# Opening of an attention-and-experts kernel: order of the first loads, constant products on TensorE, an early Sqrt, and quad 0 before quad 1's statistics

## The chip, the cores and the metric

The kernel runs on one core of a Trainium2 chip. The core has five engines that run their own instruction streams and meet at semaphores: TensorE (PE, with its weight loads shown as PEld), VectorE (DVE), ScalarE (ACT), GpSimd (POOL) and SyncE (SP, which here only issues loads and stores). The metric is device time in microseconds (us); the median of several executions counts.

## What is computed

One pre-norm transformer layer on x of shape (4, 1024, 128), float32: attention without softmax, then a mixture of 16 experts of which each token takes one, beside a shared expert.

```python
x = x + attn(layernorm(x))      # q, k l2-normed per head (16 heads of 8)
#   sim = q k^T / n**sigmoid(m[head]);  out = (sim v) Wo + bo
x = x + ffn(layernorm(x))       # router: top 1 of 16, score = sigmoid(top logit)
#   routed: (up * silu(gate)) down of the chosen expert; shared: silu(h Wg) * (h Wu) Wd
```

Since there is no softmax, (q k^T) v is computed as q (k^T v): a 128x128 matrix per sequence, masked to its head blocks.

## The kernel before

The 4096 rows are 32 tiles of 128 rows, and four tiles make a quad (8 quads, `Q = 4`). Everything stays in SBUF. Each engine has its own list of calls, in an order written out by hand; a call waits for the semaphores of what it reads or overwrites, and nothing behind it on its engine can pass it. So the order of the lists is the schedule.

The opening has these steps; c is the quad, h the half of it (two tiles).

- Loads. SP issues, per quad, `xT` (x transposed, for the products, L231) and `xres` (rows of x, for the statistics and the residual, L232), and after those of quad 0 the bias rows `b_qkv` (L234); behind the eight quads come the shared expert's weights. ACT issues `m_col` (L441), `w_qkv` (a centring matrix and Wq, Wk, Wv side by side, L442), `w_o` (L443), `bo_in` (L444) and `rwT`, the router (L445).
- Head scaling. ACT takes an Exp of `m_col` (L449), DVE two small steps (L923, L924), ACT a second Exp (L451). DVE's `scale_mask` (L909) multiplies it into `head_mask`.
- Centred weights. PE's `center_weights` (L1119) multiplies the centring matrix with the weights as soon as `w_qkv` has landed, and ACT copies the product to `w_c` (L454).
- Statistics. DVE's `x_stats(c)` (L726, L729) gives mean and variance per row, ACT's `std_x(c)` (L460) the root, DVE's `x_scales(c)` (L739) its reciprocal.
- Projection. PE's `project(c, h)` (L1135) multiplies two tiles of `xT` by `w_c` into two of four PSUM banks; one float32 product is two passes in the trace. DVE's `take(c, h)` (L764) scales them by the row's factor, adds `b_qkv` and writes `qkv`. The next quad's half can be projected only when the take of the same half has emptied its banks.
- Head norms. ACT's `square(c)` (L492), DVE's `head_sums(c)` (L772), ACT's `head_norms(c)` (L496, L500), DVE's `inv_norms(c)` (L777). Then POOL scales v and q (`scale_v`, `scale_q`, L322), and PE forms k^T v (`v_by_k`, L1144) and turns q (`turn_q`, L1161). `qkv` has two slots, so `take(2, 0)` needs both of quad 0's.

Then follow, interleaved by hand over the quads, the attention output (`fold_wo`, `attend`), the second layer norm, the router, the ranks of the rows within their expert (`choose`, `place`), POOL's scatter of the rows to DRAM by expert, the gather of 48 tiles of expert rows, the experts' products, POOL's scatter back, and the shared expert, which fills gaps to the end.

The call lists around the change, before it: ACT runs `std_x(0)`, `std_x(1)`, `square(0)`, `std_x(2)`, `head_norms(0)`, `square(1)`, `head_norms(1)` (L550 to L556). DVE runs `x_stats(0)`, `bias_rows`, `scale_mask`, `x_stats(1)`, `x_scales(0)`, `take(0, 0)`, `x_scales(1)`, `take(0, 1)`, `x_stats(2)`, `take(1, 0)`, `head_sums(0)`, `take(1, 1)`, `x_scales(2)`, `inv_norms(0)`, `head_sums(1)`, `x_stats(3)`, `inv_norms(1)`, `take(2, 0)` (L925 to L942). PE runs `center_weights`, `project` of quads 0 to 2, `v_by_k(0)`, `turn_q(0)`, `v_by_k(1)`, `turn_q(1)`, `project(3, 0)` (L1302 to L1313).

Of the kernel before, what the change touches and what calls it, by code (L numbers as in the profile page):

```python
# [8 lines left out]
ACT = mybir.ActivationFunctionType  # L9
# [5 lines left out]
P = 128  # L15


def build_block(nc, S, x, x_t, w_in, b_in, Wo, bo, m_col_in, router_t, gate_up, down, shared_gate, shared_up,
# [4 lines left out]
    _, NT, D = x.shape  # L23
    HEADS = 16
    HD = D // HEADS
    _, E, F2 = gate_up.shape
# [26 lines left out]
    with ExitStack() as ctx:  # L53
# [62 lines left out]
        with ExitStack() as attention:  # L116
            def sb_a(name, shape, dt=F32):
                return attention.enter_context(nc.sbuf_tensor(name, shape, dt))

            qkv = sb_a("qkv", [P, QRING, Q, QKV])  # L120
            sq = sb_a("sq", [P, Q, 2 * D])
            xT = sb_a("xT", [P, T])
            qT = sb_a("qT", [P, RING, Q * P])
            ss = sb_a("ss", [P, 2, Q, 2 * HEADS])
            rn = sb_a("rn", [P, 2, Q, 2 * HEADS])
            vkm = sb_a("vkm", [P, 2, D])
            wb = sb_a("wb", [P, 2, D])
            w_qkv = sb_a("w_qkv", [P, D + QKV])
            b_qkv = sb_a("b_qkv", [P, QKV])
            w_c = sb_a("w_c", [P, QKV])  # L130
            m_col = sb_a("m_col", [P, 1])
            m_tmp = sb_a("m_tmp", [P, 4])
            head_mask = sb_a("head_mask", [P, D])
            zeros = sb_a("zeros", [P, E, W])
            w_sh = sb_a("w_sh", [P, 2, SF])
            bo_in = sb_a("bo_in", [2, D])
            bo_top = sb_a("bo_top", [2, D], F32R)
            bo_two = sb_a("bo_two", [2, Q, D], F32R)
            two_col = sb_a("two_col", [2, 1])
            ones_r = sb_a("ones_r", [2, P], F32R)  # L140
# [86 lines left out]

        @block.sync
        def _(sp):
            for c in range(NQ):  # L230
                sp.dma_start(xT[:, 512 * c:512 * c + 512], x_t[:, 512 * c:512 * c + 512]).then_inc(ld_xt[c], 16)  # L231
                sp.dma_start(xres[:, Q * c:Q * c + Q, :], x[:, Q * c:Q * c + Q, :]).then_inc(ld_x[c], 16)  # L232
                if c == 0:
                    sp.dma_start(b_qkv[:], b_in.partition_broadcast(P)).then_inc(ld_b, 16)  # L234
            sp.dma_start(w_sh[:, 0], shared_gate).then_inc(ld_sg, 16)
            sp.dma_start(w_sh[:, 1], shared_up).then_inc(ld_su, 16)

            sp.wait_ge(z_done, 2)
            heads_of = x_slots.rearrange("(e r) d -> r e d", e=E)
            sp.dma_start(heads_of[0:P], zeros[:]).then_inc(zero_st, 16)  # L240
            sp.dma_start(sdT[:], shared_down).then_inc(ld_sd, 16)
            sp.dma_start(w_gu[:], gate_up).then_inc(ld_wg, 16)
            sp.dma_start(w_dn[:], down).then_inc(ld_wd, 16)

            def load(g):
                first = slot_values(0, g, mybir.EngineType.SP, E * REG - P)
                if g == 0:
                    sp.wait_ge(zero_st, 16)
                    for landed in scat:
                        sp.wait_ge(landed, 16 * NT // 2)  # L250
                for j in range(Q):
                    sp.dma_start(xg[:, g * Q + j, :], x_slots[bass.ds(first[j], P), :]).then_inc(xg_ld[g], 16)  # L252

            def bring(c):
                if c == 0:
                    for turn, landed in enumerate(y_sent):
                        sp.wait_ge(landed, 16 * len(range(turn, SLOTS, 3)))
                sp.dma_start(y_rows[:, Q * c:Q * c + Q, :], by_place[:, Q * c:Q * c + Q, :]).then_inc(y_ld[c], 16)

            sp.wait_ge(table_rdy, 1)  # L260
            for g in range(NG):
                load(g)
            for c in range(NQ):
                bring(c)
            for c in range(0, NQ, 2):
                sp.wait_ge(fin, c + 1)
                sp.dma_start(out[:, Q * c:Q * c + Q, :], xres[:, Q * c:Q * c + Q, :]).then_inc(out_st, 16)
            sp.wait_ge(fin, NQ + 1)
            sp.dma_start(out[:, Q * LAST + 2:NT, :], xres[:, Q * LAST + 2:NT, :]).then_inc(out_st, 16)
            sp.wait_ge(out_st, 16 * (NQ + 1))  # L270
# [168 lines left out]
        def _(act):  # L439
            a = nc.scalar  # L440
            act.dma_start(m_col[:], m_col_in).then_inc(ld_m, 16)  # L441
            act.dma_start(w_qkv[:], w_in).then_inc(ld_wa, 16)  # L442
            act.dma_start(w_o[:], Wo).then_inc(ld_wo, 16)  # L443
            act.dma_start(bo_in[:], bo.partition_broadcast(2)).then_inc(ld_bo, 16)  # L444
            act.dma_start(rwT[:], router_t).then_inc(ld_rw, 16)  # L445

            act.wait_ge(ld_m, 16)
            act.wait_ge(k_col, 1)
# [1 line left out]
            act.wait_ge(m_step, 1)  # L450
            a.activation(m_tmp[:, 3:4], m_tmp[:, 2:3], ACT.Exp, bias=zero_col[:],  # L451
                         scale=-float(np.log(S))).then_inc(ach, 1)
            act.wait_ge(wc_mm, 1)
            a.copy(w_c[:], pair[:, 0, 0:QKV]).then_inc(wc_rdy, 1)  # L454
            act.wait_ge(k_id, 1)

            def std(dst, mv, var, done, c):
                t = slice(Q * c, Q * c + Q)
# [3 lines left out]
            def std_x(c):  # L462
                std(rs1, mv1, var1, std1, c)
# [24 lines left out]
            def square(c):  # L488
                act.wait_ge(qkv_sb, 2 * (c + 1))
                if c >= 1:  # L490
                    act.wait_ge(ssum, c)
                a.activation(sq[:], qkv[:, c % QRING, :, 0:2 * D], ACT.Square).then_inc(sq_done, 1)  # L492

            def head_norms(c):
                act.wait_ge(ssum, c + 1)
                a.activation(ss[:, c % 2], ss[:, c % 2], ACT.Relu, bias=floor_neg[:], scale=1.0).then_inc(floored, 1)  # L496
                if c >= 2:
                    act.wait_ge(q_rdy, c - 1)
                act.wait_ge(floored, c + 1)
                a.activation(rn[:, c % 2], ss[:, c % 2], ACT.Sqrt, bias=floor_col[:], scale=1.0).then_inc(nrm, 1)  # L500
# [47 lines left out]
                a.copy(yg[:, g % YRING], ps_yg[:].rearrange("p (j d) -> p j d", d=D)).then_inc(yg_rdy, 1)  # L548

            std_x(0)  # L550
            std_x(1)
            square(0)
            std_x(2)
            head_norms(0)
            square(1)
            head_norms(1)  # L556
            qT_copy(0)
# [157 lines left out]
        def _(dve):  # L715
# [16 lines left out]
            def x_stats(c):  # L732
                dve.wait_ge(ld_x[c], 16)
                stats(c, st1, mv1, var1)
# [190 lines left out]
            x_stats(0)  # L925
            bias_rows()
            scale_mask()
            x_stats(1)
            x_scales(0)
            take(0, 0)  # L930
            x_scales(1)
            take(0, 1)
            x_stats(2)
            take(1, 0)
            head_sums(0)
            take(1, 1)
            x_scales(2)
            inv_norms(0)
            head_sums(1)
            x_stats(3)  # L940
            inv_norms(1)
# [171 lines left out]
        @block.tensor  # L1113
        def _(pe):
            te = nc.tensor

            def center_weights():
                pe.wait_ge(ld_wa, 16)
# [171 lines left out]
            def down_experts(g, after=None):  # L1290
# [8 lines left out]
                                   stop=True)  # L1299
                mm.then_inc(e_dn_mm, 1)  # L1300

            center_weights()  # L1302
            project(0, 0, after=(wc_rdy, 1))
            project(0, 1)
            project(1, 0, after=(qkv_sb, 1))
# [219 lines left out]
```

## Time and profile before

| | us |
|---|---|
| median of 3 runs (213.49 to 215.41) | 214.48 |
| the profiled execution, whole | 215.95 |
| its span, first to last instruction | 214.0 |

The profile is one execution. Its span leaves out about 2 us that lie around it, and its whole time is 0.7% over the median. Over the span PE is busy 90%, DVE 69%, ACT 48% and POOL 52%, but the share changes from stage to stage: what an edit is worth is read from its own stage.

### The profile page before, as it was taken

The numbers are of one execution on the slowest core, as the hardware profiler recorded it, in microseconds if no ns is written. First come the engines' busy times: TensorE is split into PE (matmuls) and PEld (weight loads), VectorE is DVE, ScalarE is ACT, GpSimd is POOL, SyncE is SP. The second block draws the span as 40 slices with busy tenths as digits, with TensorE's granted clock in tenths as the row PEclk, the third lists the DMA queues.
The fourth block names the chain that finished last, engine by engine and source line by source line (L and its number), as shares of the span: only waits on it lengthen the run. The fifth ranks groups of instructions, "written<-read, shape, count | busy, mean of one in ns | idle before, by whom it ended". The sixth has DMA issues, their size and how long they took to land.

```text
span 214.0 us, 3828 instructions
## 1 busy us (share of the span) xinstructions
PE 191.9 (90%) x1126; PEld 155.4 (73%) x1126; DVE 146.9 (69%) x502; ACT 103.0 (48%) x234; POOL 112.2 (52%) x140
## 2 busy tenths in 40 slices
PE   0597599999989899999888999999999999979994
PEld 0253466665768576798767988899999898869883
DVE  4759999999999977866726577856635334236555
ACT  3315265793658299683412558546653222222230
POOL 6000703347599876668740057757777778770000
PEclk9999999999999999999999999999999999999999
DMA  5999991000110011111124446621110110008525
GB/s 167 311 390 261 217 420 54 3 2 12 39 40 26 25 37 40 39 45 42 50 53 112 101 122 159 157 63 43 39 42 29 44 47 12 1 7 276 212 85 209
DMA packets 17751, 21.59 MB, mean 101 GB/s; under 512 B 3240, under 2 KB 11951, under 8 KB 17476
## 3 DMA queue, kind: packets, MB, share of 16 engines
q1 hardware_dynamic: 14016, 15.87, 25.6%
q0 software_dynamic: 2560, 4.24, 6.2%
q10 hardware_dynamic: 1156, 1.26, 1.7%
q8 instruction: 9, 0.15, 0.3%
q14 instruction: 10, 0.08, 0.1%
HBM read 13.95 MB, written 8.44 MB: 105 GB/s over the span
## 4 chain that ended last, share of the span: by engine, by line
PE 34%; DVE 27%; POOL 13%; issue 9%; DMA 9%; SPq 5%; ACT 1%; POOLq 1%; ACTq 0%; DVEq 0%
DVE qkv L764 7%; POOL y_back L357 7%; PE quad_banks L1279 6%; POOL x_slots L348 5%; SPq L252 4%; PE bank L1298 4%; DMA x_slots<-h_rows,pos 4%; DVE ss L772 4%; DVE st L726 4%; PE bank L1242 3%; DMA w_qkv<-w_in 3%; PE quad_banks L1220 3%; PE quad_banks L1222 3%; PE quad_banks L1221 3%; PE quad_banks L1135 2%
## 5 line engine op out<-in xcount | busy, mean ns | idle before, releaser
L357 POOL DMA_INDIRECT y_back<-yg,xg x48 | 47.3, 986 | 31.0 <-ACT yg L548 16.6
L849 DVE TENSOR_TENSOR s_act<-quad_banks,sg_act 128x512 f32<-128x512 f32 x32 | 22.0, 689 | 27.6 <-PE bank L1242 13.8
L520 ACT ACTIVATE sg_act<-quad_banks 128x512 f32<-128x512 f32 x32 | 19.2, 599 | 44.0 <-PE quad_banks L1222 44.0
L348 POOL DMA_INDIRECT x_slots<-h_rows,pos x32 | 31.7, 991 | 12.8 <-issue 6.3
L322 POOL TENSOR_TENSOR qkv<-qkv,rn 128x512 f32<-128x512 f32 x16 | 17.1, 1080 | 29.2 <-DVE rn L777 29.0
L1242 PEld LDWEIGHTS bank<-sdT,s_act 128*128 128x128 f32 x224 | 28.0, 191 | 1.5
L1242 PE MATMUL bank<-sdT,s_act 128*128 128x128 f32 x224 | 28.9, 275 | 0.0
L1135 PE MATMUL quad_banks<-w_c,xT 128*128 128x384 f32 x64 | 25.5, 533 | 2.1 <-DVE qkv L764 1.3
L1279 PE MATMUL quad_banks<-w_gu,xgT 128*128 x96 | 22.9, 382 | 0.8 <-ACT xgT L531 0.8
L1135 PEld LDWEIGHTS quad_banks<-w_c,xT 128*128 128x128 f32 x64 | 12.2, 208 | 11.2 <-issue 3.8
L1279 PEld LDWEIGHTS quad_banks<-w_gu,xgT 128*128 128x128 f32 x96 | 17.3, 190 | 2.9 <-issue 1.0
L764 DVE SCALAR_TENSOR_TENSOR qkv<-quad_banks,rs,b_qkv 128x384 f32<-128x384 f32 x32 | 17.7, 603 | 2.2 <-PE quad_banks L1135 2.2
L539 ACT ACTIVATE eg_act<-quad_banks,esc 128x128 f32<-128x128 f32 x48 | 13.7, 371 | 9.5 <-PE quad_banks L1279 8.7
L895 DVE SCALAR_TENSOR_TENSOR e_act<-quad_banks,esc,eg_act 128x128 f32<-128x128 f32 x48 | 13.5, 344 | 6.9 <-ACT eg_act L539 6.9
L1220 PE MATMUL quad_banks<-hT,sgT 128*128 128x512 f32 x32 | 14.8, 462 | 2.8 <-DVE s_act L849 1.6
L726 DVE BATCH_NORM_STATS2 st<-xres 128x6 f32<-128x128 f32 x64 | 13.7, 276 | 1.3 <-DMA xres<-L_attn_x 1.2
L476 ACT ACTIVATE h_rows<-xres,nm,rs 128x128 f32<-128x128 f32 x32 | 13.2, 484 | 2.0 <-DVE nm L750 2.0
L904 DVE COPY e_actT<-bank 128x512 f32<-128x512 f32 x12 | 8.3, 689 | 7.7 <-PE bank L1287 7.7
L332 POOL TENSOR_TENSOR hT<-hT_full,hT 128x512 fp32r<-128x512 f32 x8 | 10.7, 1356 | 3.8 <-ACT hT L486 3.7
L1298 PEld LDWEIGHTS bank<-w_dn,e_actT 128*128 128x128 f32 x96 | 12.3, 191 | 0.5
L1298 PE MATMUL bank<-w_dn,e_actT 128*128 x96 | 12.7, 275 | 0.0
L1221 PE MATMUL quad_banks<-hT,suT 128*128 128x512 f32 x32 | 12.6, 395 | 0.0
(146 smaller groups left out, 373.5 us busy)
## 6 DMA issues: line engine op xcount, KB each, us to landing
xg<-x_slots SPq DMA_DIRECT2D x48, 65.0 KB, 1.9
xT<-x_t SPq DMA_DIRECT2D x8, 256.0 KB, 6.8
xres<-L_attn_x SPq DMA_DIRECT2D x8, 256.0 KB, 7.0
w_gu<-gate_up SPq DMA_DIRECT2D x1, 2048.0 KB, 14.0
h_rows<-y_back SPq DMA_DIRECT2D x8, 256.0 KB, 5.3
x_slots<-zeros SPq DMA_DIRECT2D x1, 1040.0 KB, 15.4
w_dn<-down SPq DMA_DIRECT2D x1, 1024.0 KB, 15.9
out<-xres SPq DMA_DIRECT2D x4, 256.0 KB, 2.4
```

The source lines that it names most:

```text
L348: g.indirect_dma_start(out=x_slots, out_offset=bass.IndirectOffsetOnAxis(ap=pos[:, t:t + 1], axis=0), in_=h_rows[:, t, :], in_offset=None) ...
L357: nc.gpsimd.indirect_dma_start(out=y_back, out_offset=bass.IndirectOffsetOnAxis(ap=xg[:, n, D + 1:D + 2].bitcast(I32), axis=0), in_=yg[:, ...
L520: a.activation(sg_act[:, n % 2], pair[:, 2 * (n % 2)], ACT.Silu).then_inc(s_silu, 1)
L726: last = v.bn_stats(st[:, t, :], xres[:, t, :])
L764: last = v.scalar_tensor_tensor(out=qkv[:, c % QRING, j, :], in0=pair[:, j, 0:QKV], scalar=rs1[:, t:t + 1], in1=b_qkv[:], op0=ALU.mult, op ...
L849: v.tensor_tensor(s_act[:, n % 2], pair[:, 2 * (n % 2) + 1], sg_act[:, n % 2], ALU.mult).then_inc(s_act_rdy, 1)
L1135: last = te.matmul(pair[:, j, 0:QKV], xT[:, P * (Q * c + j):P * (Q * c + j + 1)], w_c[:], start=True, stop=True)
L1220: te.matmul(to, lhs[:, 0], rhs[:, 0], start=True, stop=False)
L1221: te.matmul(to, lhs[:, 0], rhs[:, 1], start=False, stop=False)
L1242: last = te.matmul(Y_BANK[c][:, here], s_act[:, n % 2, here], sdT[:, D * k:D * k + D], start=(k == 0 and j == 0), stop=(k == KC - 1 and j ...
L1279: mm = te.matmul(gate_up_banks(g % 2)[:, j, :], xgT[:, g % 2, P * j:P * j + P], gu_cols[:, bass.ds(held[g][j] * 2, F2)], start=True, stop= ...
L1298: mm = te.matmul(ps_yg[:, here], e_actT[:, g % 2, here], dn_cols[:, bass.ds(cols[j], D)], start=True, stop=True)
```

## The change

- SP issues `w_qkv` first and no longer `b_qkv`. ACT issues `m_col`, then `b_qkv` and `bo_in`; it issues `w_o` and `rwT` only behind the copy of `w_c`.
- ACT calls a Sqrt of one column, whose value nothing reads, behind its second Exp and ahead of the copy of `w_c`. `m_tmp` is one column wider for it. The wait for `k_id` moves with it.
- PE multiplies `ones` by `ones` into a bank that nothing uses yet: four products before `center_weights`, one behind it. It waits for `k_pool`, the memsets, first.
- ACT's `square(0)` comes ahead of `std_x(1)`, and `head_norms(0)` ahead of `std_x(2)`.
- DVE takes quad 0 ahead of `x_stats(1)`; `head_sums(0)`, `take(1, 0)`, `inv_norms(0)` and `take(1, 1)` come ahead of `x_stats(2)`. From `x_stats(3)` on the order is as before.

```diff
--- before.py
+++ after.py
@@ -129,7 +129,7 @@
             b_qkv = sb_a("b_qkv", [P, QKV])
             w_c = sb_a("w_c", [P, QKV])
             m_col = sb_a("m_col", [P, 1])
-            m_tmp = sb_a("m_tmp", [P, 4])
+            m_tmp = sb_a("m_tmp", [P, 5])
             head_mask = sb_a("head_mask", [P, D])
             zeros = sb_a("zeros", [P, E, W])
             w_sh = sb_a("w_sh", [P, 2, SF])
@@ -227,11 +227,10 @@
 
         @block.sync
         def _(sp):
+            sp.dma_start(w_qkv[:], w_in).then_inc(ld_wa, 16)
             for c in range(NQ):
                 sp.dma_start(xT[:, 512 * c:512 * c + 512], x_t[:, 512 * c:512 * c + 512]).then_inc(ld_xt[c], 16)
                 sp.dma_start(xres[:, Q * c:Q * c + Q, :], x[:, Q * c:Q * c + Q, :]).then_inc(ld_x[c], 16)
-                if c == 0:
-                    sp.dma_start(b_qkv[:], b_in.partition_broadcast(P)).then_inc(ld_b, 16)
             sp.dma_start(w_sh[:, 0], shared_gate).then_inc(ld_sg, 16)
             sp.dma_start(w_sh[:, 1], shared_up).then_inc(ld_su, 16)
 
@@ -439,10 +438,8 @@
         def _(act):
             a = nc.scalar
             act.dma_start(m_col[:], m_col_in).then_inc(ld_m, 16)
-            act.dma_start(w_qkv[:], w_in).then_inc(ld_wa, 16)
-            act.dma_start(w_o[:], Wo).then_inc(ld_wo, 16)
+            act.dma_start(b_qkv[:], b_in.partition_broadcast(P)).then_inc(ld_b, 16)
             act.dma_start(bo_in[:], bo.partition_broadcast(2)).then_inc(ld_bo, 16)
-            act.dma_start(rwT[:], router_t).then_inc(ld_rw, 16)
 
             act.wait_ge(ld_m, 16)
             act.wait_ge(k_col, 1)
@@ -450,9 +447,12 @@
             act.wait_ge(m_step, 1)
             a.activation(m_tmp[:, 3:4], m_tmp[:, 2:3], ACT.Exp, bias=zero_col[:],
                          scale=-float(np.log(S))).then_inc(ach, 1)
+            act.wait_ge(k_id, 1)
+            a.activation(m_tmp[:, 4:5], zero_col[:], ACT.Sqrt, bias=eps_col[:], scale=1.0)
             act.wait_ge(wc_mm, 1)
             a.copy(w_c[:], pair[:, 0, 0:QKV]).then_inc(wc_rdy, 1)
-            act.wait_ge(k_id, 1)
+            act.dma_start(w_o[:], Wo).then_inc(ld_wo, 16)
+            act.dma_start(rwT[:], router_t).then_inc(ld_rw, 16)
 
             def std(dst, mv, var, done, c):
                 t = slice(Q * c, Q * c + Q)
@@ -548,10 +548,10 @@
                 a.copy(yg[:, g % YRING], ps_yg[:].rearrange("p (j d) -> p j d", d=D)).then_inc(yg_rdy, 1)
 
             std_x(0)
+            square(0)
             std_x(1)
-            square(0)
+            head_norms(0)
             std_x(2)
-            head_norms(0)
             square(1)
             head_norms(1)
             qT_copy(0)
@@ -925,17 +925,17 @@
             x_stats(0)
             bias_rows()
             scale_mask()
-            x_stats(1)
             x_scales(0)
             take(0, 0)
+            take(0, 1)
+            x_stats(1)
+            head_sums(0)
             x_scales(1)
-            take(0, 1)
+            take(1, 0)
+            inv_norms(0)
+            take(1, 1)
             x_stats(2)
-            take(1, 0)
-            head_sums(0)
-            take(1, 1)
             x_scales(2)
-            inv_norms(0)
             head_sums(1)
             x_stats(3)
             inv_norms(1)
@@ -1114,6 +1114,10 @@
         def _(pe):
             te = nc.tensor
 
+            def warm(n):
+                for _ in range(n):
+                    te.matmul(ps_log[:, 0:P], ones[:], ones[:], start=True, stop=True)
+
             def center_weights():
                 pe.wait_ge(ld_wa, 16)
                 te.matmul(pair[:, 0, 0:QKV], w_qkv[:, 0:D], w_qkv[:, D:D + QKV], start=True, stop=True
@@ -1299,7 +1303,10 @@
                                    stop=True)
                 mm.then_inc(e_dn_mm, 1)
 
+            pe.wait_ge(k_pool, 1)
+            warm(4)
             center_weights()
+            warm(1)
             project(0, 0, after=(wc_rdy, 1))
             project(0, 1)
             project(1, 0, after=(qkv_sb, 1))
```

## Rows read from the trace of the kernel before

**Rows 1.** Windows: us, busy of PE, PEld, DVE, ACT, POOL, granted clock, DMA share, GB/s.

```profile
14.00:24.55 10.55, 8.21 (x30) 4.18 (x28) 9.64 (x28) 4.48 (x8) 2.12 (x2) 1.00 1.19 254
24.55:74.80 50.25, 46.36 (x249) 32.96 (x250) 48.72 (x179) 30.22 (x68) 30.04 (x30) 1.00 0.21 79
```

**Rows 2.** Chain of waits: start us, us, what.

```profile
1.25 5.93 DMA w_qkv<-w_in
```

**Rows 3.** Timeline of ACT: start, us, engine, line, operation, tiles, count, [idle before, releaser].

```profile
5.25 0.29 ACT L451 ACTIVATE m_tmp<-m_tmp,zero_col 128x1 f32<-128x1 f32 x1 [0.42 <-DVE m_tmp L924]
...
8.91 0.48 ACT L454 COPY w_c<-quad_banks 128x384 f32<-128x384 f32 x1 [3.37 <-PE quad_banks L1119]
9.40 1.28 ACT L460 ACT_TABLE_LOAD   x1
10.70 0.49 ACT L460 ACTIVATE rs<-mv,eps_col 128x4 f32<-128x4 f32 x2
...
15.79 1.06 ACT L492 ACTIVATE sq<-qkv 128x1024 f32<-128x1024 f32 x1 [4.60 <-DVE qkv L764]
```

**Rows 4.** Timeline of PE, in narrow windows so that single passes show.

```profile
7.22 1.65 PE L1119 MATMUL quad_banks<-w_qkv 128*128 128x384 f32 x2 [7.22 <-DMA w_qkv<-w_in]
9.53 0.98 PE L1135 MATMUL quad_banks<-w_c,xT 128*128 128x384 f32 x1 [0.66 <-ACT w_c L454]
...
12.86 1.39 PE L1135 MATMUL quad_banks<-w_c,xT 128*128 128x384 f32 x2
13.50 1.07 PE L1135 MATMUL quad_banks<-w_c,xT 128*128 128x384 f32 x2
14.09 0.81 PE L1135 MATMUL quad_banks<-w_c,xT 128*128 128x384 f32 x2
...
25.73 1.16 PE L1144 MATMUL bank<-qkv 128*128 128x128 f32 x8 [1.69 <-POOL qkv L322]
26.77 0.66 PE L1161 MATMUL bank<-ident,qkv 128*128 128x128 f32 x4
27.26 1.46 PE L1135 MATMUL quad_banks<-w_c,xT 128*128 128x384 f32 x4
```

**Rows 5.** Timeline of DVE up to the first take.

```profile
5.31 0.87 DVE L726 BATCH_NORM_STATS2 st<-xres 128x6 f32<-128x128 f32 x4
...
6.83 0.21 DVE L914 CAST ones_r<-ones 2x128 fp32r<-2x128 f32 x1 [0.23 <-DMA bo_in<-L_attn_bo]
...
8.13 0.27 DVE L909 TENSOR_SCALAR head_mask<-head_mask,m_tmp 128x128 f32<-128x128 f32 x1
...
11.03 0.18 DVE L739 RECIPROCAL rs<-rs 128x4 f32<-128x4 f32 x1 [0.17 <-ACT rs L460]
12.57 1.14 DVE L764 SCALAR_TENSOR_TENSOR qkv<-quad_banks,rs,b_qkv 128x384 f32<-128x384 f32 x2 [1.36 <-PE quad_banks L1135]
```

**Rows 6.** Timeline of DVE from the second take of quad 0 on.

```profile
14.62 1.14 DVE L764 SCALAR_TENSOR_TENSOR qkv<-quad_banks,rs,b_qkv 128x384 f32<-128x384 f32 x2 [0.82 <-PE quad_banks L1135]
15.68 0.86 DVE L726 BATCH_NORM_STATS2 st<-xres 128x6 f32<-128x128 f32 x4
...
16.87 1.11 DVE L764 SCALAR_TENSOR_TENSOR qkv<-quad_banks,rs,b_qkv 128x384 f32<-128x384 f32 x2
17.89 1.21 DVE L772 TENSOR_REDUCE ss<-sq 128x128 f32<-128x1024 f32 x1
...
23.61 0.92 DVE L777 RECIPROCAL rn<-rn 128x128 f32<-128x128 f32 x1
24.55 1.14 DVE L764 SCALAR_TENSOR_TENSOR qkv<-quad_banks,rs,b_qkv 128x384 f32<-128x384 f32 x2
```

**Rows 7.** Timeline of SP's queue, the first issue.

```profile
0.81 0.39 SPq L231 DMA_DIRECT2D xT<-x_t  x1
```

**Rows 8.** By line, L231: the landing of that load.

```profile
DMA to landing us min/median/max: 3.3/3.3/3.3
```

## The prediction

> **What bounds the kernel now.** I read the windows first, then the timeline of each engine over the opening, then the landing of the loads. From the start of take(2,0) at 24.55 us to 74.80 us VectorE (DVE) is busy 48.72 of 50.25 us [rows 1]. Whatever reaches VectorE in that stretch earlier or later moves what follows by nearly as much, and the order behind take(2,0) is not edited. At that point both orders have done the same VectorE work. So the change is worth the shift of the start of take(2,0), and I call it S.
>
> The opening before 24.55 has two parts. Up to the first take at 12.57 us VectorE waits: w_qkv lands at 1.25 + 5.93 = 7.18 us [rows 2], TensorE centres the weights, ScalarE (ACT) copies w_c at 8.91, and the products of quad 0 start at P0 = 9.53 [rows 3, 4]. The first take starts 3.04 us behind P0 and the second 5.09 us behind it (14.62) [rows 5, 6]. From the end of that second take, where the next operation starts at T = 15.68, VectorE is almost solid, and take(2,0) starts 8.87 us later [rows 6].
>
> The products of quad 0 run slow. One pass of 384 columns starts 0.64 us behind the other (12.86, 13.50), while from 14.09 on, and later (four in 1.46 us), the pace is about 0.32 us [rows 4]. The granted-clock column reads 1.00 over both stretches [rows 1], so it is the pace that tells the level: 1.2 GHz up to about 14.0 us and 2.4 GHz after. Before that rise TensorE had worked without a pause since 9.53, that is for some 4.5 us.
>
> **The change part by part.**
>
> *Weights first on SP.* The first xT load, as large as w_qkv, was issued at 0.81 [rows 7] and landed 3.3 us later [rows 8]; from that place w_qkv lands at about 4.1. The centre product takes 1.65 us [rows 4] and is ready at about 5.8. xT and xres of quad 0 each move one place back on SP, while xT of quad 1 and all that follow keep their place, since b_qkv leaves the third. b_qkv goes second on ACT's queue.
>
> *When xres of quad 0 lands.* Call this Lx. Before, x_stats(0) started at 5.31 [rows 5], so it had landed by then; a later place gains nothing, and 5.3 is the lower bound. The upper one is 7.2, the landing of w_qkv, which had the second place on the other queue [rows 2]. I take the middle, 6.3, as the new third place lies between. Behind it VectorE needs x_stats(0) 1.29 (5.31 to 6.60, as 6.83 follows 0.23 of idle), bias_rows 1.30, scale_mask 0.27 and x_scales(0) 0.18 [rows 5]: VectorE is free for the first take at about Lx + 3.1 = 9.4 (8.4 to 10.3).
>
> *Root table early.* ScalarE's second Exp ends at 5.25 + 0.29 = 5.54. Now the table load of Sqrt follows it: 1.28 us, to 6.83, and the small Sqrt some 0.2 before the next instruction can start (two of them take 0.49) [rows 3]. The copy of w_c stands behind both, so it starts at about 7.05, although its product is ready at 5.8. P0 follows the copy's start by 0.62 (8.91 to 9.53) [rows 3, 4]: the new P0 is 7.67, and not the 6.45 that the weights would allow. An Exp up to 0.2 earlier would take as much off. The load is only moved: it stood at 9.40, beside products that the first take had to await anyway, so 1.2 us of the gain is spent here. A landing of w_qkv anywhere up to 5.3 gives the same P0. The Trainium skill's "ScalarE: Activation LUTs", section "What ACT_TABLE_LOAD costs", counts 1.28 us for the load and 1.38 us more for a drain. By that rule P0 would be 9.05 and the sum below 216.4; the trace does not agree, since the load starts 0.01 us behind the copy and the next instruction 0.02 us behind the load [rows 3], and I go by the trace.
>
> *Loads moved behind the copy.* ScalarE issues w_o and rwT before std_x(0), at about 0.4 us each by an issue on SP [rows 7], so std_x(0) starts near 8.4. This is hidden by VectorE's bias_rows and scale_mask, which run to about 9.2; both loads are first needed behind take(2,0). Without that cover it costs 0.8. SP issues as many loads as before.
>
> *Constant products.* Four products on ones, then one behind the centre product. Their 128 columns are a third of the 384 of a pass, so by the slow pace a pass takes 0.21 us and four products of two passes 1.7 us. They fill 1.7 to 3.5 us, before w_qkv lands, and the fifth fits into the wait for the copy. They cost nothing; the question is whether they raise the clock. After them TensorE stands idle from about 6.0 to 7.67. I take the row of before: idle or in pieces until the projections, then about 4.5 us at the slow rate, and the products of quad 0 as far behind P0 as they were.
>
> *The new order of VectorE.* take(0,0) then starts at 7.67 + 3.04 = 10.7, take(0,1) at 7.67 + 5.09 = 12.76, and T is 13.8. Behind T, with steps from start to start [rows 6]: x_stats(1) 1.19, head_sums(0) 1.13, x_scales(1) 0.1, take(1,0) 1.04, inv_norms(0) 0.93, take(1,1) 1.04, x_stats(2) 1.19, which is 6.62. square(0), 1.06 [rows 3], is done under x_stats(1), and head_norms(0) under take(1,0): each of its two steps has 128 columns, so it takes no longer than the w_c copy's 0.48 on 384 [rows 3]. Now VectorE waits: std_x(2) can start only after x_stats(2), and ScalarE's square(1) stands behind std_x(2) although its input has been ready for 1.2 us. std_x(2) starts at about 6.73, square(1) at 6.95 and ends at 8.0, so head_sums(1) starts at 8.04. Then 1.13, x_stats(3) 1.2 and inv_norms(1) 0.94: take(2,0) starts at T + 11.3. Before it was T + 8.87. Of the 2.4 more, 1.2 is x_stats(1), which used to fill the wait for the products, 0.1 x_scales(1), and 1.1 the new wait.
>
> **Sum.** S = (13.8 + 11.3) - 24.55 = +0.55. The break-even is T = 13.25. Against the profiled execution this is a span of 214.6 for 214.0. Its own whole time, 215.95, lies 0.7% over the median, 214.48; on the median the sum gives 215.0.
>
> **The rivals.**
>
> *The clock is up before quad 0's products.* Then the products are ready at P0 + 1.5 and P0 + 2.8, VectorE becomes the bound at Lx + 3.1, and T is 11.6 (at the earliest 11.55, by the second half; with Lx = 7.2 it is 12.4). S is -1.65, from -1.7 to -0.85: 212.8, up to 213.6. For it: TensorE would be at work for about 3.8 of the 4.2 us from 1.7 to 5.9. Against it: the pause to 7.67, and that 1.65 us of centre product did not do it before. By the Trainium skill's "TensorE: Matmul & The Clock Gate", Part 1, the slow clock is the default and sustained activity releases it; the trace agrees as far as the rise at 14.0 goes.
>
> *The clock falls in a new pause (slower).* Behind project(2,1), which waits for take(1,1) and ends near T + 7.05, TensorE has v_by_k(0), 1.16, and turn_q(0), 0.66 [rows 4], and is idle from about T + 8.9. v_by_k(1) follows the end of inv_norms(1) by 1.18 (24.55 to 25.73), so it starts at T + 12.5: a pause of 3.6 us, where before it was 1.69 and four passes behind it still took 1.46 [rows 4]. If the clock falls there, the work of the next 4.5 us (v_by_k(1), turn_q(1), project(3)) runs at half pace and loses at most 2.25, less some slack: with +0.55 that is 216.0 to 217.3, say 216.8. It decides only if the clock falls in that pause; it did not in the one of 1.69, and no row here shows a longer one after the rise.
>
> *The early landing fails (slower).* If ACT's and SP's loads share so that w_qkv lands at 7.18 as before, P0 stays 9.53, T is 15.7 and S +2.4: 216.9. It decides from a landing at 5.3 on. Against it stands the xT load from the same place.
>
> **How the numbers follow.** The forecast, with the clock rising during quad 0's products, has 0.52. If the rise comes 1.5 us earlier, T is 0.75 less; if it comes only after them, T is about 0.5 more: 214.3 to 215.6. The early clock has 0.28, the pause 0.10, the late landing 0.04, and 0.06 is left for what I don't see, on either side. The range leaves out the outer ends: 212.8, the low end of the early clock, to 216.6. A change of 1%, or 2.1 us, is about what a measurement of this kernel can tell from none. Faster than 212.3 needs more than the early clock gives by the sum: 0.10. Slower than 216.6 is the larger part of the pause and the late landing: 0.10. Within 1%: 0.80.
>
> **What the profile will show.** Right: w_qkv's centre product at 4.1 to 4.3; ScalarE's table load between 5.4 and 6.9 and the w_c copy right behind it; P0 near 7.7; passes 0.64 apart in quad 0's first half; square(1) behind std_x(2), with two idle stretches of VectorE of 0.4 and 0.8 us; take(2,0) near 25.1. Wrong: 0.32 us passes from the start with take(2,0) near 23; or slow passes again behind the pause; or a w_c copy that does not wait for the table.

## The result and the profile after

| | before | after |
|---|---|---|
| median of 4 executions, us | 214.94 (213.49 to 215.5) | 217.82 (216.89 to 218.17) |
| the profiled execution, whole | 215.95 | 216.89 |
| its span | 214.0 | 215.0 |
| start of take(2,0) in it | 24.55 | 24.92 |

The ratio after to before is 1.0138, 95% interval 1.0073 to 1.0202: the change made the kernel slower by 2.9 us. A second set of after, beside other executions of before, gave 217.8 and 1.013 (1.0051 to 1.0209). Forecast were 215.0 and a range up to 216.6. The profiled execution of before was one of its slower ones and that of after its fastest, so the two spans show 1.0 of the 2.9. In the comparisons below single executions that lie over 1.5% above the fastest of their kernel are left out of the ratio; medians are over all.

The page of after, two lines: the span, and the granted clock in 40 slices of 5.4 us.

```profile
span 215.0 us, 3848 instructions
PEclk9889979999999999999999999999999999999999
```

The clock falls twice, around 9 and around 26 us; before it stood at 1.00 in the stretches of [rows 1]. The windows of after, columns as in [rows 1]:

```profile
4.00:7.00 3.00, 1.83 (x4) 1.03 (x4) 0.32 (x2) 2.47 (x5) 0.43 (x5) 1.00 0.67 170
...
9.00:12.00 3.00, 3.00 (x6) 1.33 (x4) 2.80 (x15) 0.30 (x1) 0.00 (x0) 0.50 1.07 396
...
24.00:26.00 2.00, 0.00 (x0) 0.00 (x0) 2.00 (x7) 0.51 (x2) 0.92 (x1) 1.00 1.15 247
26.00:28.00 2.00, 1.79 (x8) 1.79 (x9) 1.97 (x11) 0.30 (x1) 1.19 (x2) 0.50 1.01 404
28.00:30.00 2.00, 2.00 (x9) 1.65 (x8) 1.75 (x11) 0.82 (x2) 0.00 (x0) 0.65 0.99 418
```

TensorE does nothing from 24 to 26 us, and the clock is at half (1.2 GHz) right behind it. TensorE's timeline (start, us, engine, line, operation; in brackets the idle time before and what ended it):

```profile
1.80 2.08 PE L1119 MATMUL bank<-ones 128*128 128x128 f32 x8 [1.80 <-POOL seen L284]
3.93 1.65 PE L1123 MATMUL quad_banks<-w_qkv 128*128 128x384 f32 x2
5.37 0.45 PE L1119 MATMUL bank<-ones 128*128 128x128 f32 x2
...
7.93 1.93 PE L1139 MATMUL quad_banks<-w_c,xT 128*128 128x384 f32 x4 [2.10 <-DMA xT<-x_t]
...
9.01 3.40 PE L1139 MATMUL quad_banks<-w_c,xT 128*128 128x384 f32 x5
...
21.59 0.60 PE L1165 MATMUL bank<-ident,qkv 128*128 128x128 f32 x4
26.21 2.08 PE L1148 MATMUL bank<-qkv 128*128 128x128 f32 x8 [4.02 <-POOL qkv L321]
28.08 1.06 PE L1165 MATMUL bank<-ident,qkv 128*128 128x128 f32 x4
```

The constants and the centre product run ahead of 6 us, as planned, and the first products of quad 0 are fast: three passes from 7.93 to 9.01, 0.36 us each. From 9.01 on it is five in 3.40, 0.68 each. Later comes the pause, 4.02 us, and behind it `v_by_k(1)` takes 2.08 us for the 1.16 of before and `turn_q(1)` 1.06 for 0.66 [rows 4]. VectorE's timeline:

```profile
8.71 0.87 DVE L726 BATCH_NORM_STATS2 st<-xres 128x6 f32<-128x128 f32 x4 [3.95 <-DMA xres<-L_attn_x]
...
11.63 2.19 DVE L764 SCALAR_TENSOR_TENSOR qkv<-quad_banks,rs,b_qkv 128x384 f32<-128x384 f32 x4
13.74 0.86 DVE L726 BATCH_NORM_STATS2 st<-xres 128x6 f32<-128x128 f32 x4
...
20.81 0.18 DVE L739 RECIPROCAL rs<-rs 128x4 f32<-128x4 f32 x1 [0.36 <-ACT rs L460]
21.75 1.22 DVE L772 TENSOR_REDUCE ss<-sq 128x128 f32<-128x1024 f32 x1 [0.77 <-ACT sq L492]
...
24.92 1.04 DVE L764 SCALAR_TENSOR_TENSOR qkv<-quad_banks,rs,b_qkv 128x384 f32<-128x384 f32 x2
...
30.75 1.22 DVE L772 TENSOR_REDUCE ss<-sq 128x128 f32<-128x1024 f32 x1 [0.81 <-ACT sq L492]
31.89 1.66 DVE L764 SCALAR_TENSOR_TENSOR qkv<-quad_banks,rs,b_qkv 128x384 f32<-128x384 f32 x3
```

The first statistics wait till 8.71 for `xres` (5.31 before, [rows 5]); take(2,0) is 0.37 late against [rows 6]; take(3,0) starts at 31.89, so behind the slow stretch it is 1.44 late against this row of before:

```profile
30.45 2.18 DVE L764 SCALAR_TENSOR_TENSOR qkv<-quad_banks,rs,b_qkv 128x384 f32<-128x384 f32 x4
```

ScalarE's timeline, which answers to [rows 3]; ACTq is its queue of loads:

```profile
5.11 1.28 ACT L451 ACT_TABLE_LOAD   x1
5.62 0.35 ACTq L454 DMA_DIRECT2D w_o<-L_attn_Wo  x1
6.01 0.78 ACTq L455 DMA_DIRECT2D rwT<-router_t  x1
6.41 0.29 ACT L451 ACTIVATE m_tmp<-zero_col,eps_col 128x1 f32<-128x1 f32 x1
6.61 0.46 ACT L453 COPY w_c<-quad_banks 128x384 f32<-128x384 f32 x1
```

### The profile page after: what moved, and what is told of

It reads as the page before. It is cut to its first block, busy times and chain, and to the rows that moved or that the text cites. A ratio compares the mean times of both kernels' runs of the same rounds, so it can differ in the third digit from the quotient of the medians.

```text
span 215.0 us, 3848 instructions
## 1 busy us (share of the span) xinstructions
PE 194.8 (91%) x1136; PEld 158.7 (74%) x1136; DVE 146.2 (68%) x502; ACT 103.2 (48%) x235; POOL 112.2 (52%) x140
## 4 chain that ended last, share of the span: by engine, by line
PE 42%; DVE 13%; POOL 13%; DMA 11%; issue 8%; SPq 6%; ACT 1%; POOLq 0%; DVEq 0%
DMA x_slots<-h_rows,pos 10%; PE bank L1246 7%; POOL x_slots L347 7%; PE quad_banks L1283 6%; PE quad_banks L1224 5%; SPq L251 5%; PE quad_banks L1226 5%; PE quad_banks L1225 5%; PE bank L1302 4%; POOL qkv L321 4%; DVE qkv L764 3%; DVE st L726 3%; PE bank L1291 2%; PE bank L1257 2%; DVE ss L772 2%
## 5 line engine op out<-in xcount | busy, mean ns | idle before, releaser
L356 POOL DMA_INDIRECT y_back<-yg,xg x48 | 47.3, 985 | 29.2 <-ACT yg L548 13.9
L1139 PE MATMUL quad_banks<-w_c,xT 128*128 128x384 f32 x64 | 25.2, 527 | 4.8 <-DVE qkv L764 2.5
L1139 PEld LDWEIGHTS quad_banks<-w_c,xT 128*128 128x128 f32 x64 | 11.9, 203 | 13.0 <-issue 5.8
L764 DVE SCALAR_TENSOR_TENSOR qkv<-quad_banks,rs,b_qkv 128x384 f32<-128x384 f32 x32 | 17.5, 598 | 0.2
L726 DVE BATCH_NORM_STATS2 st<-xres 128x6 f32<-128x128 f32 x64 | 13.8, 277 | 4.2 <-DMA xres<-L_attn_x 4.0
L1224 PE MATMUL quad_banks<-hT,sgT 128*128 128x512 f32 x32 | 14.8, 463 | 1.5 <-DVE s_act L849 1.4
L1148 PE MATMUL bank<-qkv 128*128 128x128 f32 x64 | 9.5, 296 | 4.0 <-POOL qkv L321 4.0
L1226 PE MATMUL quad_banks<-hT,sgT 128*128 128x512 f32 x32 | 12.7, 396 | 0.0
```

What stands on the lines that cost most here:

```text
L356: nc.gpsimd.indirect_dma_start(out=y_back, out_offset=bass.IndirectOffsetOnAxis(ap=xg[:, n, D + 1:D + 2].bitcast(I32), axis=0), in_=yg[:, ...
L726: last = v.bn_stats(st[:, t, :], xres[:, t, :])
L764: last = v.scalar_tensor_tensor(out=qkv[:, c % QRING, j, :], in0=pair[:, j, 0:QKV], scalar=rs1[:, t:t + 1], in1=b_qkv[:], op0=ALU.mult, op ...
L1139: last = te.matmul(pair[:, j, 0:QKV], xT[:, P * (Q * c + j):P * (Q * c + j + 1)], w_c[:], start=True, stop=True)
L1224: te.matmul(to, lhs[:, 0], rhs[:, 0], start=True, stop=False)
L1226: return te.matmul(to, lhs[:, 1], rhs[:, 0], start=False, stop=True)
```

## The experiments

Two theories. The pause theory: take(2,0) comes about as late as the sum said, and the loss is the clock that falls in the pause of 4.02 us ahead of `v_by_k(1)`, which the new call order of VectorE made. The loads theory: the loss comes from the opening's loads, which land late (`xres` at 8.71). Both can hold, for different parts of the time.

All twelve, each beside the kernel before on the same chip; e1 to e4, e5 to e8 and e9 to e12 are three sets on three chips, so rows of different sets are best compared by their ratios to before. e5 is after once more. The pause is what remains of it where constants fill it. "Clock" is the mean granted clock of each execution: a recorded slow stretch such as the one from 26 to 30 us above takes off (0.50 x 2 + 0.35 x 2) / 215 = 0.008, so the figure counts the falls, wherever in the span they lie. It does not price them: before itself has at least one (0.990 to 0.992) in 18 of its 57 executions, and in e1 the three executions with one (214.19 to 215.00) are faster than the median of the other seven (215.68).

| kernel | median us | ratio to before (95%) | take(2,0) | pause ahead of v_by_k(1) | clock |
|---|---|---|---|---|---|
| after | 217.82 | 1.0138 (1.0073 to 1.0202) | 24.92 | 4.02 | 0.976 to 0.990 |
| e1_fill_pause | 215.12 | 1.0043 (1.0010 to 1.0076) | 24.87 | 0.90 | 0.998 and above in 7 of 10 |
| e2_calls_back | 215.79 | 1.0062 (1.0023 to 1.0101) | 23.63 | 1.69 | 0.998 and above in 5 of 10 |
| e3_loads_back | 215.62 | 1.0051 (1.0012 to 1.0089) | 24.39 | 2.79 | 0.983 to 0.992 |
| e4_bias_third | 212.41 | 0.9898 (0.9831 to 0.9965) | 22.24 | 2.68 | 0.976 to 0.992 |
| e5_after_again | 217.80 | 1.0130 (1.0051 to 1.0209) | 24.73 | 4.02 | 0.984 to 0.992 |
| e6_bias_rows | 216.14 | none | 24.03 | 2.79 | 0.976 to 0.992 |
| e7_calls_only | 218.70 | 1.0151 (1.0058 to 1.0244) | 25.68 | 4.02 | 0.976 to 0.992 |
| e8_all_three | 210.80 | 0.9816 (0.9719 to 0.9912) | 21.55 | 1.79 | 1.000, one 0.990 |
| e9_no_const | 218.06 | 1.0209 (1.0144 to 1.0274) | 25.74 | 4.02 | 0.976 to 0.991 |
| e10_bias_calls_back | 213.75 | 0.9989 (0.9952 to 1.0025) | 21.99 | 1.69 | below 0.993 in 7 of 10 |
| e11_no_fill | 214.14 | 0.9992 (0.9957 to 1.0027) | 21.39 | 1.91 | 0.984 to 0.992 |
| e12_calls_back_fill | 212.53 | 0.9901 (0.9861 to 0.9941) | 21.86 | 0.57 | 0.998 and above in 6 of 10 |

### The pause, filled

After, with 14 more constant products between `turn_q(0)` and `v_by_k(1)`.

```diff
             turn_q(0)
+            warm(14)
             v_by_k(1)
```

> The changed kernel with 14 more products of ones on TensorE between turn_q(0) and v_by_k(1), about 3.1 us of the 4.0 us pause at the fast rate. Theory PAUSE (the clock falls to 0.50 in that pause, and the half-rate stretch from 26.0 to 29.3 us is what was lost): granted clock 1.00 from 24 to 32 us, v_by_k(1) in about 1.1 us for 2.08, take(3,0) near 31.0 for 31.89, time 1.0 to 2.0 us under the changed kernel (216 to 217). Rival LOADS (the late landing of quad 0's xT and xres is the loss) and rival ORDER (the new call order of VectorE costs it by itself): clock or not, the time stays within 0.5 us of the changed kernel's 217.8.

TensorE's timeline of this kernel:

```profile
21.97 3.29 PE L1119 MATMUL bank<-ones 128*128 128x128 f32 x28
26.16 1.16 PE L1148 MATMUL bank<-qkv 128*128 128x128 f32 x8 [0.90 <-POOL qkv L321]
27.19 0.66 PE L1165 MATMUL bank<-ident,qkv 128*128 128x128 f32 x4
```

The added products compute nothing that is used, and 2.7 us come back by the medians (217.82 to 215.12), 2.0 by the ratios; 1.0 to 2.0 was expected. All ten executions (at most 216.72) are faster than all eight of after (at least 216.89). take(2,0) starts at 24.87 and `v_by_k(1)` at 26.16, both as late as in after, so nothing ahead of them has moved; it takes 1.16 us again, and take(3,0) starts at 30.67 for 31.89. This is the cleanest verdict of the study: the lost clock behind the pause is most of what made the change slow. What is left, +0.9 us by the ratio, is near the S of 0.55 that the sum gave.

### The call lists, taken back and taken alone

After with before's lists of DVE and ACT:

```diff
+            x_stats(1)
             x_scales(0)
             take(0, 0)
-            take(0, 1)
-            x_stats(1)
-            head_sums(0)
             x_scales(1)
...
```

> The changed kernel with the call lists of VectorE and ScalarE as before; its loads, constant products and early Sqrt stay. PAUSE: TensorE's pause ahead of v_by_k(1) is back at about 1.7 us, the clock stays up behind it, take(2,0) starts near 23.9 (x_stats(0) still late, at 8.7, then x_stats(1) ahead of the first take, T near 15.0, plus 8.9); time 214 to 215.2, some 3 us under the changed kernel. LOADS: x_stats(0) still starts at 8.7, so the time stays at 217 or more. ORDER: as PAUSE in time, but then the first run of this set (the filled pause) gains nothing.

And the other way round, before with only the new lists:

> The kernel before with nothing but the new call lists of VectorE and ScalarE. From the steps: T near 15.7 as before, then 11.2 to 11.3 to take(2,0), for 8.9: near 27, and a pause of TensorE of some 4 us ahead of v_by_k(1), with a recorded fall of the clock in most runs: 217.5 to 219.5, 3 to 5 us over before. If the constant products were needed for a fall, the clock stays at 1.00 and the time at 216.5 to 217.2.

The new lists alone make before slower by 1.5%: take(2,0) comes 1.1 us later, and they bring the pause of 4.02 and the half clock behind it (0.79 from 26 to 28 us, 0.50 from 28 to 30). So with before's loads that part of the change hurts. Taking it back did not bring all of it back, though: 215.79, above the 214 to 215.2 expected. TensorE's timeline of after with before's lists:

```profile
22.50 0.63 PE L1165 MATMUL bank<-ident,qkv 128*128 128x128 f32 x4
24.82 1.26 PE L1148 MATMUL bank<-qkv 128*128 128x128 f32 x8 [1.69 <-POOL qkv L321]
25.87 1.10 PE L1165 MATMUL bank<-ident,qkv 128*128 128x128 f32 x4
26.76 2.64 PE L1139 MATMUL quad_banks<-w_c,xT 128*128 128x384 f32 x4
```

Here the clock falls behind a pause of 1.69 us, the very length that left it up in before [rows 4]: four passes take 2.64, not 1.46. Five of the ten executions show no fall (median 215.0) and five do (216.5). So one profile with a pause and no fall did not show that such a pause is safe.

### The loads

After with before's order of loads on SP and ACT:

```diff
-            sp.dma_start(w_qkv[:], w_in).then_inc(ld_wa, 16)
...
+                if c == 0:
+                    sp.dma_start(b_qkv[:], b_in.partition_broadcast(P)).then_inc(ld_b, 16)
...
-            act.dma_start(b_qkv[:], b_in.partition_broadcast(P)).then_inc(ld_b, 16)
+            act.dma_start(w_qkv[:], w_in).then_inc(ld_wa, 16)
+            act.dma_start(w_o[:], Wo).then_inc(ld_wo, 16)
...
```

> The changed kernel with the loads on the queues and in the order of before; its call lists, constant products and early Sqrt stay. LOADS: quad 0's xT and xres land at 4 to 5.5 us again and the time comes back to 215 or less. PAUSE: w_qkv lands near 7.2, the projections start near 9.5, take(2,0) comes at 25.5 to 27, TensorE's pause of about 4 us and the half-rate stretch behind it stay; time 217.8 to 219.5, no better than the changed kernel.

2.2 us faster than after (1.9 by the ratios), so the new order of loads is no gain as it stands. The time lies between the two that were expected, and it does not separate the theories: take(2,0) is 0.5 us earlier than in after, take(3,0) 1.7, and the 1.2 between them is the clock, which stays up behind a pause of 2.79. TensorE's and then VectorE's timeline:

```profile
25.68 1.16 PE L1149 MATMUL bank<-qkv 128*128 128x128 f32 x8 [2.79 <-POOL qkv L322]
```

```profile
24.39 1.04 DVE L765 SCALAR_TENSOR_TENSOR qkv<-quad_banks,rs,b_qkv 128x384 f32<-128x384 f32 x2
...
30.19 2.18 DVE L765 SCALAR_TENSOR_TENSOR qkv<-quad_banks,rs,b_qkv 128x384 f32<-128x384 f32 x4
```

`w_qkv` landed at 5.5 us here, with the queues of before, where the profile of before has 7.18 [rows 2]; e7, with the same queues, has 5.6. The clock fell too, between 17 and 21 us, in quad 2's products, which the takes reach later: take(2,0) follows T by 11.17 us, as in after (11.18), so a fall there cost VectorE nothing up to that point.

The next one undoes a single line of the load order: `b_qkv` goes back to SP, behind quad 0's `xT` and `xres`, while `w_qkv` stays first.

```diff
                 sp.dma_start(xres[:, Q * c:Q * c + Q, :], x[:, Q * c:Q * c + Q, :]).then_inc(ld_x[c], 16)
+                if c == 0:
+                    sp.dma_start(b_qkv[:], b_in.partition_broadcast(P)).then_inc(ld_b, 16)
...
-            act.dma_start(b_qkv[:], b_in.partition_broadcast(P)).then_inc(ld_b, 16)
```

> The changed kernel with one load moved: b_qkv (a row broadcast to 128 partitions) is issued by SP behind quad 0's xT and xres, and no longer second by ACT. If the broadcast holds up what lands beside it: xT of quad 0 lands near 5.3 for 7.9, xres near 6 for 8.7, the projections start near 7.1 (behind the table load and the copy of w_c), take(2,0) 1 to 2 us earlier than 24.9. If it is only a matter of places in the queues, xT and xres gain less than 0.7 us. LOADS then sees the time at 215.5 or less; PAUSE sees the pause and the half-rate stretch stay and the time at 216 to 217.

TensorE's and then VectorE's timeline of it (one line added, so L1140 for L1139, L727 for L726, L765 for L764):

```profile
7.14 5.77 PE L1140 MATMUL quad_banks<-w_c,xT 128*128 128x384 f32 x16 [1.26 <-ACT w_c L454]
```

```profile
5.80 0.87 DVE L727 BATCH_NORM_STATS2 st<-xres 128x6 f32<-128x128 f32 x4 [1.11 <-DMA xres<-L_attn_x]
...
11.06 0.86 DVE L727 BATCH_NORM_STATS2 st<-xres 128x6 f32<-128x128 f32 x4
...
22.24 1.04 DVE L765 SCALAR_TENSOR_TENSOR qkv<-quad_banks,rs,b_qkv 128x384 f32<-128x384 f32 x2
...
28.04 2.18 DVE L765 SCALAR_TENSOR_TENSOR qkv<-quad_banks,rs,b_qkv 128x384 f32<-128x384 f32 x4
```

`xres` lands 2.9 us earlier (5.80), take(2,0) comes 2.7 earlier, and the kernel is 5.4 us faster than after (5.1 by the ratios) and 1.0% faster than before. That rests on three executions (212.07 to 212.47); the fourth took 217.56, at a clock of 0.976. Not all of the gain is the loads' own: take(3,0) is 3.9 us earlier than in after, and the 1.2 beyond the 2.7 is the fall, which is no longer there behind a pause of 2.68. The rest is not traced. Now the products wait for the copy of `w_c`, behind the table load, as the prediction had it; in after they waited for `xT`. A load of 192 KB that nothing needed before the first take (11.63 in after) had delayed those that everything waited for.

Is it the bytes or their pattern? `b_qkv` is one row of 1.5 KB that the load reads 128 times, once for each partition. In the next kernel it is laid out in DRAM as 128 equal rows, and its load stands where it stands in after, with the same bytes.

```diff
-            act.dma_start(b_qkv[:], b_in.partition_broadcast(P)).then_inc(ld_b, 16)
+            act.dma_start(b_qkv[:], b_in).then_inc(ld_b, 16)
```

> The changed kernel with b_qkv laid out in DRAM as 128 equal rows, so that its load reads 192 KB of different addresses, from the same place in the queue, in place of one row 128 times. Theory BROADCAST (reading one row 128 times is what is slow and holds up its neighbours): the moved GB/s from 4 to 7 us go from 170 to 300 or more, xT of quad 0 lands at 5.0 to 6.2 for 7.9, take(2,0) 1.5 to 2.7 us earlier than 24.9, time 213 to 215.5. Rival PLACE (any 192 KB there do the same): xT lands at 7.3 or later, and the time stays at 217 or more.

The loads issued from 0.5 to 2.5 us, first of after, then of this kernel (KB each, us from issue to landing), and then this kernel's window that answers to the 170 GB/s of after:

```profile
xres<-L_attn_x SPq DMA_DIRECT2D x1, 256.0 KB, 7.0
b_qkv<-b_in ACTq DMA_DIRECT2D x1, 192.0 KB, 6.8
```

```profile
xres<-L_attn_x SPq DMA_DIRECT2D x1, 256.0 KB, 4.5
b_qkv<-b_in ACTq DMA_DIRECT2D x1, 192.0 KB, 4.1
```

```profile
4.00:7.00 3.00, 2.08 (x4) 1.18 (x4) 1.11 (x6) 2.21 (x5) 0.41 (x5) 1.00 1.03 368
```

It is the pattern. With distinct rows `b_qkv` lands after 4.1 us, not 6.8, its neighbour `xres` after 4.5, not 7.0, and all queues together move 368 GB/s in these three microseconds, not 170 (five profiles with the broadcast in this place lie between 170 and 192). As a time this kernel tells little (213 to 215.5 was expected): two executions took 214.3 and 214.5, two 217.8 at a clock of 0.976, and in its profile quad 0's products ran slow again, so that take(2,0) stands at 24.03.

### The constants

After without its constant products:

```diff
-            pe.wait_ge(k_pool, 1)
-            warm(4)
             center_weights()
-            warm(1)
```

> The changed kernel without its constant products. If they are of little account where quad 0's xT lands at 7.9: the first products run slow, T moves from 13.7 to about 14.1, the pause ahead of v_by_k(1) stays and so does a recorded fall: 217.3 to 218.7 us. If they are what buys the falls (a clock raised early, then lost in the wait for xT): mean granted clock 0.992 or more in all runs and 215.5 to 217.

The window of this kernel that answers to 9 to 12 us of after:

```profile
9.00:12.00 3.00, 3.00 (x6) 1.49 (x6) 2.81 (x15) 0.30 (x1) 0.00 (x0) 1.00 1.07 395
```

Quad 0's products start at the same place, 8.00, and are slow from the first pass on, though the column reads 1.00; T is 14.56, 0.8 later than in after, and take(2,0) 25.74. So the constants do raise the clock ahead of the products, against what the prediction took. In time it is not to be told from after: the two intervals overlap. The late `xres` holds VectorE back either way, and the pause of 4.02 is there in both.

### All three, and what each is worth

`b_qkv` third on SP as above, `square(1)` ahead of `std_x(2)` on ScalarE, and short runs of constants in the three waits of TensorE:

```diff
-            std_x(2)
             square(1)
+            std_x(2)
...
-            warm(1)
+            warm(3)
             project(0, 0, after=(wc_rdy, 1))
...
+            warm(6)
             project(2, 0, after=(qkv_sb, 3))
...
+            warm(6)
             v_by_k(1)
```

> The changed kernel with b_qkv behind quad 0's loads on SP, square(1) ahead of std_x(2) on ScalarE, and constant products in TensorE's pauses: three for one behind center_weights, six ahead of project(2,0), six ahead of v_by_k(1). By the steps: take(2,0) 0.7 to 0.9 us ahead of the run that only moved b_qkv (22.24), so near 21.4, and granted clock 1.00 from 7 to 32 us: 210.5 to 212, under both kernels. If the wait for square(1) or the falls were of no account, it stays at 212 to 212.8.

This is the fastest kernel of the study, 210.8: 1.8% under before, 7.0 us under after, by three executions (210.59 to 210.88); the fourth took 215.07, with a fall. The same without the added constants:

> The run with all three edits, without its added constant products: b_qkv behind quad 0's loads, and square(1) ahead of std_x(2). take(2,0) near 21.5. If the fills matter (the clock falls in the pauses of about 2 us otherwise), granted clock 0.976 to 0.992 and 211.3 to 213; if only the order counts, the 210.8 of the full set.

One window of e8_all_three and then of e11_no_fill:

```profile
16.00:20.00 4.00, 3.80 (x23) 2.65 (x23) 3.60 (x15) 1.72 (x3) 2.00 (x2) 1.00 1.14 325
```

```profile
16.00:20.00 4.00, 4.00 (x13) 2.25 (x12) 3.60 (x16) 1.84 (x4) 1.84 (x2) 0.61 1.15 302
```

Without them take(2,0) is just as early (21.39), but every execution has at least one fall, and the gain is gone: 0.9992, where at most 213 us was expected. The two profiles differ by less, 211.54 and 210.59: there the one fall lies in quad 2's products, where little waits (take(2,0) follows T by 10.30 us with it and by 10.29 without). It was the fastest of the ten executions of e11. Where the clock falls in the slower ones no profile shows, so that the constants bring the gain is shown, and by which fall it is lost without them is not.

Last, the same treatment with before's call lists, first without and then with constants in the waits:

> The changed kernel with b_qkv behind quad 0's loads on SP, and with the call lists of before. x_stats(0) near 5.8; x_stats(1), ahead of the first take, waits for quad 1's xres near 9.8, so T near 13.5, and take(2,0) 8.9 later near 22.4, about where the run that only moved b_qkv had it (22.24). If the new lists are worth something once the loads land early, this one is 1 us or more slower than that run's 212.4; by the steps it is 212 to 213.5, no worse, with fewer falls of the clock as its pause ahead of v_by_k(1) is 1.7 us for 2.7.

> b_qkv behind quad 0's loads and the call lists of before, with constant products in TensorE's pauses (three for one behind center_weights, four ahead of project(2,0), five ahead of v_by_k(1)). Granted clock 1.00, take(2,0) near 22.4: 211.5 to 212.8. Against the 210.8 of all three edits it tells what the new lists with square(1) put right are worth: by the steps 0.9 us.

Seven of ten executions of the first show a fall, and it equals before (0.9989), although take(2,0) is 2.6 us earlier. It is 1.3 us slower than e4, which by its expectation speaks for the new lists once the loads land early, but e4 has four executions and the intervals overlap. With constants it is 0.9901; in its ten executions those without a fall have a median of 212.2, those with one 214.2. The one that was profiled (213.44) has its only fall far behind the opening; two windows and two rows of TensorE's timeline:

```profile
82.00:83.00 1.00, 1.00 (x2) 0.40 (x3) 0.90 (x8) 1.00 (x1) 0.70 (x2) 0.81 0.20 67
83.00:84.00 1.00, 1.00 (x3) 0.35 (x2) 0.90 (x5) 0.47 (x2) 0.68 (x2) 0.50 0.17 58
```

```profile
80.93 1.06 PE L1196 MATMUL bank<-rwT,hT_full 128*128 128x16 f32 x8 [0.26 <-ACT hT_full L483]
...
82.34 1.84 PE L1174 MATMUL bank<-xres,ident 128*128 128x512 f32 x2
```

The longest wait of TensorE in the 8 us ahead of it is 0.26 us, and before, e8 and e10 run the same products behind the same wait without a fall. So not every fall follows a pause, and the constants in the opening do not reach this one. The intervals of e8 and e12 overlap, so whether the new lists, mended, are better than the old ones is not settled. Not tried: e4 without the early Sqrt, and before with only `b_qkv` moved.

## Why the prediction was wrong

**The failed step: the chance of the pause.** The prediction named the mechanism that decided, its place and its price (a pause of 3.6 us ahead of `v_by_k(1)`, 216.8), and gave it 0.10, because the clock had not fallen in a pause of 1.69. So its sum has no term for the lost clock, which e1 measures at 2.0 us by the ratios and 2.7 by the medians. The pause was 4.02, and both profiles of after, e7 and e9 show the fall behind it. Even the ground it stood on was one execution: e2 shows a fall behind 1.69. The Trainium skill's "TensorE: Matmul & The Clock Gate", section "HAM oscillation — how this bites in real kernels", says that a wait between two groups of products can throttle the engine again, so that the next group starts slow; the trace agrees, with 0.50 behind the pause. Part 1 of that page of the Trainium skill says of the rise that it is "run-variable"; here the fall is too (e2, five of ten). The length of the pause alone does not tell, though: behind 2.68 us in e4 and 2.79 in e3 and e6 the column stayed at 1.00, and behind 4.02 it fell in four profiles of four. What decides stays open. With one execution to judge by, and a pause twice as long to come, this rival deserved at least an even chance.

**The size of the fall.** "At most 2.25, less some slack": the trace has +0.37 at take(2,0) and +1.44 at take(3,0), so 1.1 by then, and POOL's sixteenth scatter starts at 83.81 in after and 82.28 with the pause filled, 1.5 later. The ratios give 2.0, the medians 2.7. The part beyond 1.5 is not traced: in the profile of after the next scatter waits 1.74 us for an earlier one to land and that of e1 does not, but the profile of before has such a wait too (1.71), so it need not come from the change.

**The landing of xres (mis-sized).** Lx was put at 5.3 to 7.2 and measured 8.7; `xT` held P0 to 7.93. The bound took the second place on the other queue for the worst that could happen, and did not ask what `b_qkv`, moved ahead of them, does to its neighbours: the 128-fold read of one row halved what all queues moved. Undone in e4, Lx is 5.80, inside the bounds.

**T right by two errors.** 13.8 was forecast, by slow products; 13.74 came, by a late `xres` and VectorE's own work behind it. The products were fast at first, as the early-clock rival has it, and its own sum, Lx + 5.2 (12.4 for 7.2), gives 13.9 for the true Lx. In e4, where Lx is early, T is 11.06, where that sum gives 11.0, and take(2,0) 22.24. So the rival was the truer picture of the opening, spoilt by one load.

**From T to take(2,0).** Right: 11.18 us for 11.3, with the two waits at 0.36 and 0.77 for 0.4 and 0.8. Moving `square(1)` ahead of `std_x(2)` makes it 10.29 in e8 (11.26 to 21.55), as the naming of that wait says.

**The table load.** `w_qkv` had landed by 3.93, when the centre product starts (4.1 forecast), the copy of `w_c` starts at 6.61 and ends at 7.07, behind the load and the small Sqrt. Right as a mechanism, but P0 waits for `xT`; in e4 it binds, and P0 is 7.14.

**The loads behind the copy.** Wrong in the working, without effect: `w_o` and `rwT` were issued at 5.62 and 6.01, as soon as the centre product was done (3.93 + 1.65 = 5.58) and while ScalarE still loaded its table; they did not hold `std_x(0)` back, which waited for the late statistics. So for loads it does not hold that nothing can pass a call ahead of it on its engine: these two passed the copy, once the wait ahead of it was met.

**The base.** The 7.18 at which `w_qkv` landed in before was the time of that execution; the same queues gave 5.5 and 5.6 in e3 and e7. Part of the gain that the early weights were to bring was not there to be had.

## What to carry to other kernels

When a new order lengthens a wait of TensorE, price the products behind it at half clock before anything else, and do not take one profile without a fall as a proof: look at the mean granted clock of several executions, which tells that a fall came, and at profiles, which tell where. Cheap constant products in the waits mostly hold the clock (no fall in 16 of 24 executions of e1, e8 and e12, for 3 of 20 of e10 and e11), but they pay only where the work behind them is what others wait for. A load that reads one row for all partitions belongs behind the loads that the opening waits for, or its rows laid out one by one.

## What the runs showed of the hardware

- One DRAM row of 1.5 KB read for 128 partitions held all queues together to 170 GB/s from 4 to 7 us; 128 equal rows of the same size in its place let them move 368, and the neighbouring 256 KB load landed after 4.5 us and not 7.0.
- The clock fell behind a pause of 4.02 us in each profile that has one (after, e5, e7, e9), and behind 1.69 in e2. It did not behind 1.69 in before and e10, nor behind 2.68 and 2.79 in e4, e3 and e6. In these three it had fallen some microseconds earlier, in quad 2's products; in e4, e3 and e6 these follow idle times of 1.98, 2.05 and 2.08, and in after and e7 they follow 1.84 and 2.14 without a fall. In e12 it fell at 82.6 us, behind a wait of 0.26. What decides is open.
- The granted-clock column shows falls but not the slow start: in e9 it reads 1.00 from 9 to 12 us, while six passes fill these 3.00 us, 0.5 each or slower.
- ScalarE's queue issued two loads that stand behind the copy of `w_c` in its list 1.0 and 0.6 us before that copy started.
